# High table parts kept in PSUM for the subtraction, and part of the one-hot work of the first supertile given to ScalarE, in a recommendation-model tower on one core

## The chip, the core and the metric

The kernel runs on one core of a Trainium2 chip. TensorE (PE) does the matmuls, VectorE (DVE) and ScalarE (ACT) the elementwise work and the moves out of PSUM, GpSimd (POOL) gathers table rows with indirect DMAs, and SyncE (SP) issues most other DMAs. The metric is the device time of one execution in microseconds, the median of three runs.

## The reference

A batch of 2048 samples looks up one row of 128 numbers in each of 27 tables. All pairs of the 27 rows are multiplied (351 dot products), 16 dense values are appended, and three layers follow.

```
e = jnp.stack([tbl_0[ids[:, 0]], ..., tbl_26[ids[:, 26]]], axis=1)
dot = jnp.einsum('bnd,bmd->bnm', e, e)          # the 351 pairs are kept as z
h = jnp.concatenate([z, dense_ctx], axis=1)
h = jnp.maximum(h @ W_top1 + b_top1, 0.0)
h = jnp.maximum(h @ W_top2 + b_top2, 0.0)
y = h @ W_top3
```

## The kernel before

The batch is cut into NS = 4 supertiles of ST = 4 tiles of 128 samples. Ten small tables (eight of 1000 rows, two of 1250, the "hot" ones, numbered h = 0 to 9) are looked up on TensorE, for a whole supertile at a time: a table lies in SBUF with its rows on 125 partitions in 8 or 10 chunks, VectorE makes a one-hot matrix of 125x512 for each chunk (`tensor_scalar`, `is_equal`, L478), and TensorE multiplies the chunk with it (L664, L666). To keep fp32 accuracy a table is held as two parts of the type fp32r: `table_hi`, the table rounded by a cast on ScalarE (`split_high`, L527), and `table_lo`, the table minus `table_hi`, a `tensor_tensor` on VectorE (`split_low`, L444). Both are made once, in the first supertile, between the lookups. An eleventh table ("half", h = 10) is looked up in the same way with one-hots of 256 columns (L460, L681, L682), in the first two supertiles only. The other 16 tables (17 later on) are gathered on GpSimd, one indirect DMA for a table and tile (L434), into one of NR = 3 buffers; the gathers of tile k+3 wait for TensorE's transposes of tile k.

In a tile, TensorE transposes the gathered rows (L692), ScalarE and VectorE copy them into `eT` (L574, L494), TensorE forms the products of the pairs (L710) in four banks, `products(n, t, 0)` in the two `ps_hot` banks and `products(n, t, 1)` in the two `ps_dot` banks, and VectorE and ScalarE copy the banks out (L231). Layers of earlier tiles are woven in (L723, L745, L766).

What sets the order is the program text of each engine, with counting semaphores between engines:

- In the first supertile VectorE does for each hot table `split_low(h)` and then its 8 or 10 one-hots; it may be NO = 4 one-hots ahead of TensorE (`onehot_used`).
- ScalarE splits tables 0 to 3 ahead of the lookups. Then it copies the result of table h out of PSUM (L582) and splits table h + 4 behind that copy. TensorE has two PSUM banks for the lookups, and waits for the copy of table h before it begins table h + 2.
- A raw table h + 4 lands in the same place as table h (`PLACE`, four places), so SyncE issues its load (L304) when `split_low(h)` is done (`lo_ready`).

## Time and profile before

| | before |
|---|---|
| median of 3 runs | 641.28 us (640.8 to 643.16) |
| the profiled execution: its time | 642.85 us |
| the profiled execution: its span | 641.0 us |
| mean granted TensorE clock | 0.787 |
| busy: PE, DVE, ACT, POOL | 404.4, 215.7, 97.9, 260.6 us |

The profiled execution is one run; its span is what the trace covers, and its time is that of the run as it is timed. A busy share is an average over the whole span, and this kernel has stretches of very different kinds: the lookups of a supertile and its four tiles.

### The profile page before, as it was taken

How to read it: one execution, taken by the hardware profiler on the slowest of the kernel's cores; microseconds unless marked ns; L12 is line 12 of the kernel's file. 1: busy time of each engine (PE TensorE's matmuls, PEld its weight loads, DVE VectorE, ACT ScalarE, POOL GpSimd, SP SyncE). 2: the span in 40 equal slices, each digit the busy share in tenths (PEclk: the TensorE clock that was granted, in tenths of full speed). 3: DMA queues.
4: the chain of work that ended last, by engine and by line, in shares of the span. 5: the costliest groups of instructions: out<-in, count | busy, mean ns of one | idle time of the engine just before them, and what ended most of it. 6: DMA issues, size and time to landing. Idle time of an engine off the chain costs nothing.

```text
span 641.0 us, 9183 instructions
## 1 busy us (share of the span) xinstructions
PE 404.4 (63%) x3768; PEld 341.8 (53%) x3768; DVE 215.7 (34%) x462; ACT 97.9 (15%) x190; POOL 260.6 (41%) x272
## 2 busy tenths in 40 slices
PE   5888315263739992819271999371808089955997
PEld 3667204152628891718161888261707078845996
DVE  6898003010109960301010797010101059801220
ACT  2442001010111210102020212010201012110322
POOL 6778763544540027363645001737273600072000
PEclk9899557585959996758685999666767579985999
DMA  8983313131414202223222230123232325010322
GB/s 224 248 213 93 82 49 69 49 81 38 97 37 91 61 13 53 55 67 62 61 62 60 49 103 8 50 44 86 39 84 45 77 34 114 9 50 23 59 48 36
DMA packets 71137, 45.23 MB, mean 71 GB/s; under 512 B 53100, under 2 KB 59628, under 8 KB 71096
## 3 DMA queue, kind: packets, MB, share of 16 engines
q1 hardware_dynamic: 60578, 25.80, 18.0%
q0 software_dynamic: 8448, 17.32, 10.7%
q10 hardware_dynamic: 2070, 1.53, 1.0%
q8 instruction: 30, 0.49, 0.3%
q14 instruction: 11, 0.09, 0.0%
HBM read 38.75 MB, written 5.87 MB: 70 GB/s over the span
## 4 chain that ended last, share of the span: by engine, by line
PE 54%; issue 33%; DVE 4%; another core or an unknown queue 3%; DMA 3%; SPq 1%; ACT 1%; ACTq 0%
PE ps_hot L710 12%; PE ps_hot L664 10%; PE ps_hot L666 9%; PE ps_h L723 6%; PE ps_dot L710 6%; PE ps_tr L692 5%; PE ps_h L745 3%; DVE onehot L478 3%; DMA dots<-in_tbl 2%; PE ps_h L766 2%; PE ps_hot L681 1%; PE ps_hot L682 1%; DVE table_lo L444 1%; DMA dots_scratch<-dots 1%
## 5 line engine op out<-in xcount | busy, mean ns | idle before, releaser
L434 POOL DMA_INDIRECT rows<-in_tbl,cold_ids x264 | 259.7, 984 | 320.6 <-PE ps_tr L692 237.9
L710 PE MATMUL ps_hot<-eT 128*54 128x54 f32 x1024 | 77.2, 261 | 214.7 <-issue 195.3
L710 PEld LDWEIGHTS ps_hot<-eT 128*54 128x54 f32 x1024 | 59.1, 171 | 232.5 <-issue 211.9
L478 DVE TENSOR_SCALAR onehot<-hot_ids,row_number 125x512 fp32r<-125x512 int32 x336 | 146.8, 485 | 4.7 <-PE ps_hot L666 2.6
L664 PE MATMUL ps_hot<-onehot,table_hi 125*128 125x512 f32 x336 | 134.2, 399 | 14.8 <-DVE onehot L478 10.9
L666 PE MATMUL ps_hot<-onehot,table_lo 125*128 125x512 f32 x336 | 132.9, 396 | 0.0
L231 DVE COPY dots<-ps_hot 128x432 f32<-128x432 f32 x16 | 9.7, 608 | 238.3 <-remote 131.7
L664 PEld LDWEIGHTS ps_hot<-onehot,table_hi 125*128 125x128 f32 x336 | 64.2, 191 | 33.1 <-issue 17.6
L666 PEld LDWEIGHTS ps_hot<-onehot,table_lo 125*128 125x128 f32 x336 | 64.2, 191 | 13.1
L494 DVE COPY eT<-ps_tr 128x512 f32<-128x512 f32 (+1 forms) x36 | 23.3, 648 | 111.6 <-remote 56.4
L723 PE MATMUL ps_h<-zT,w 128*128 128x128 f32 x360 | 50.6, 281 | 0.0
L723 PEld LDWEIGHTS ps_h<-zT,w 128*128 128x128 f32 x360 | 46.0, 197 | 0.1
L582 ACT COPY eT<-ps_hot 128x512 f32<-128x512 f32 x40 | 26.6, 665 | 107.0 <-PE ps_hot L666 107.0
L692 PE MATMUL ps_tr<-ident,rows 128*128 128x128 f32 x264 | 41.8, 280 | 0.9 <-ACT eT L574 0.7
L710 PEld LDWEIGHTS ps_dot<-eT 128*54 128x54 f32 x1024 | 37.4, 164 | 6.2 <-issue 6.1
L710 PE MATMUL ps_dot<-eT 128*54 128x54 f32 x1024 | 39.4, 249 | 1.2 <-issue 1.2
L544 ACT ACTIVATE h<-ps_h,b 128x128 f32<-128x128 f32 x30 | 9.4, 363 | 159.5 <-remote 146.8
L692 PEld LDWEIGHTS ps_tr<-ident,rows 128*128 128x128 f32 x264 | 31.3, 144 | 3.3 <-ACT eT L574 1.4
L574 ACT COPY eT<-ps_tr 128x512 f32<-128x512 f32 (+1 forms) x36 | 20.1, 559 | 65.0 <-remote 39.1
L745 PE MATMUL ps_h<-h,w 128*128 128x128 f32 x240 | 29.4, 276 | 0.4 <-ACT results L554 0.4
L745 PEld LDWEIGHTS ps_h<-h,w 128*128 128x128 f32 x240 | 28.0, 192 | 0.8 <-ACT h L539 0.7
L231 DVE COPY dots<-ps_dot 128x432 f32<-128x432 f32 x16 | 9.7, 608 | 44.4 <-PE ps_dot L710 44.4
(39 smaller groups left out, 140.0 us busy)
## 6 DMA issues: line engine op xcount, KB each, us to landing
hot_ids<-in_hot_ids SPq DMA_DIRECT2D x40, 256.0 KB
dots_scratch<-dots SPq DMA_DIRECT2D x62, 87.8 KB
rows<-in_tbl,cold_ids POOLq DMA_INDIRECT x264
zT<-dots_scratch SPq DMA_DIRECT2D x47, 58.5 KB
w<-in_tbl SPq DMA_DIRECT2D x3, 448.0 KB
dots<-in_tbl SPq DMA_DIRECT2D x2, 560.0 KB
dots<-in_tbl SPq DMA_DIRECT2D x2, 448.0 KB
w<-in_tbl SPq DMA_DIRECT2D x1, 560.0 KB
```

What stands on the lines that cost most here:

```text
L231: return copy(dots[i][:, :, BS * k:BS * k + BS], of)
L434: pool.indirect_dma_start(out=rows[k % NR][:, f, :], out_offset=None, in_=x["cold"][f][:, :], in_offset=bass.IndirectOffsetOnAxis(ap=cold_ ...
L478: dve.tensor_scalar(onehot[:, c % NO, :], hot_ids[h % NI][0:CR, :], row, None, ALU.is_equal).then_inc(onehot_ready, 1)
L494: dve.tensor_copy(eT[:, i, :, at:at + len(f), :], ps_tr[1][:, 0:len(f), :].rearrange("d f (q b) -> d q f b", b=2))\
L574: act.copy(eT[:, t % 2, :, at:at + len(f), :], ps_tr[0][:, 0:len(f), :].rearrange("d f (q b) -> d q f b", b=2)).then_inc(tr_read[0], 1)
L582: act.copy(eT[:, :, :, NC + h:NC + h + NH + 1:NH, :], ps_hot[h % 2][:, :].rearrange("d (a i q b) -> d i q a b", a=2, i=2, b=2))\
L664: pe.matmul(ps_hot[h % 2][:, :], table_hi[:, c, :], onehot[:, c % NO, :], start=(c == FROM[h]), stop=False)
L666: pe.matmul(ps_hot[h % 2][:, :], table_lo[:, c, :], onehot[:, c % NO, :], start=False, stop=(c == FROM[h + 1] - 1)).then_inc(onehot_used, 1)
L692: last = pe.transpose(ps_tr[pair][:, f - TG * g, :], rows[tile(n, t) % NR][:, f, :], ident[:, :])
L710: last = pe.matmul(banks[k][SC * c:SC * c + WN, WN * g:WN * g + WN], e.rearrange("d a b -> d (a b)"), e.rearrange("d a b -> d b a"), start ...
L723: last = pe.matmul(ps_h1[:, m, :], w1[0:k, c, m * P:(m + 1) * P], zT[i][0:k, c, :], start=(c == 0), stop=(c == KC - 1))
L745: last = pe.matmul(ps_h2[:, m, :], w2[:, c, m * P:(m + 1) * P], h1[:, c, :], start=(c == 0), stop=(c == M1 - 1))
```

## The change

1. The eight PSUM banks are declared as `ps_hot` (two banks as before) and two tensors of three banks, `ps_tr_h1` and `ps_dot_h2`; `ps_tr`, `ps_dot`, `ps_h1` and `ps_h2` are views of them. In the first supertile, whose tiles have not begun, these two serve as two places (`apart`) for the high part of a table.
2. `split_high(h)` for h > 0 casts the staged table twice: into `table_hi` in SBUF, and into `apart[h % 2]` in PSUM. `split_low(h)` for h > 0 subtracts the PSUM copy instead of the one in SBUF. The second cast waits for `split_low(h - 2)`.
3. ScalarE splits tables 0 to 2 ahead of the lookups, and table h + 3 (not h + 4) behind the copy of table h.
4. In the first supertile the one-hot of the last chunk of tables 3 to 9 is made by ScalarE (`one_hot`): `Abs` of row number minus id into `distance` (the storage of `h1`), and then `Relu` of one minus that. It stands behind the copy of table h - 1 and ahead of the split of table h + 2, and its `Relu` waits for `onehot_used` of four chunks earlier. VectorE skips these seven chunks. SyncE's loads of ids into a used buffer wait for ScalarE's read too.
5. The two memsets of `ps_dot` on VectorE, and TensorE's wait for them, are gone; the copies of the products take 118 of 128 partitions.

```
-        ps_tr = [ps(f"ps_tr{i}", [P, TG, P]) for i in range(2)]
-        ps_dot = [ps(f"ps_dot{i}", [P, ST * P]) for i in range(2)]
-        ps_h1 = ps("ps_h1", [P, M1, P])
-        ps_h2 = ps("ps_h2", [P, 4, P])
+        ps_tr_h1 = ps("ps_tr_h1", [P, 3, 4, P])
+        ps_dot_h2 = ps("ps_dot_h2", [P, 3, 4, P])
+        apart = [bank.rearrange("p a c d -> p (a c) d")[0:CR] for bank in (ps_tr_h1, ps_dot_h2)]
...
             def split_low(h, part=0):
...
-                dve.tensor_tensor(in_table(table_lo, h, part), staging[h][:, a:b], in_table(table_hi, h, part),
+                high = apart[h % 2][:, 0:CHUNKS[h]] if h else in_table(table_hi, h, part)
+                dve.tensor_tensor(in_table(table_lo, h, part), staging[h][:, a:b], high,
                                   ALU.subtract).then_inc(lo_ready, 1)
...
+                        if by_scalar(n, c):
+                            continue
...
             def split_high(h, part=0):
...
-                act.copy(in_table(table_hi, h, part), staging[h][:, a:b]).then_inc(hi_ready, 1)
+                high = act.copy(in_table(table_hi, h, part), staging[h][:, a:b])
+                if h:
+                    if h > 2:
+                        act.wait_ge(lo_ready, splits(h - 2))
+                    high = act.copy(apart[h % 2][:, 0:CHUNKS[h]].bitcast(f32r), staging[h])
+                high.then_inc(hi_ready, 1)
...
+            def one_hot(h):
+                c = FROM[h + 1] - 1
+                row = row_number[0:CR, KINDS.index(CHUNKS[h]), CHUNKS[h] - 1:CHUNKS[h]]
+                act.wait_ge(hot_ids_ready[h % NI], 16 * (ids_uses(0, h) + 1))
+                act.wait_ge(act_onehot_ready, by_scalar_before(0, c))
+                act.activation(distance, hot_ids[h % NI][0:CR, :], ACT.Abs, bias=row, scale=-1.0)\
+                   .then_inc(distance_ready, 1)
+                act.wait_ge(distance_ready, by_scalar_before(0, c + 1))
+                act.wait_ge(onehot_used, c - NO + 1)
+                act.activation(onehot[:, c % NO, :], distance, ACT.Relu, bias=1.0, scale=-1.0)\
+                   .then_inc(act_onehot_ready, 1)
...
-                    if first and h + NB < NH:
-                        split_high(h + NB)
-                    if first and h == BEFORE[NH]:
-                        split_high(NH)
+                    if first and h + 1 in BY_SCALAR:
+                        one_hot(h + 1)
+                    if first and h + NB - 1 <= NH:
+                        split_high(h + NB - 1)
```

ScalarE's instructions from the splits ahead of the lookups on, before (`ps_hot0` and `ps_hot1` are the results of even and odd tables; `dots0`, `dots1`, `w2`, `w1` are the places of the raw tables):

```order
L527 CAST table_hi<-dots1 125x1024
L527 CAST table_hi<-w2 125x1024
L527 CAST table_hi<-w1 125x1024
L582 COPY eT<-ps_hot0 128x128x2x2
L527 CAST table_hi<-dots0 125x1024
L582 COPY eT<-ps_hot1 128x128x2x2
L527 CAST table_hi<-dots1 125x1024
L582 COPY eT<-ps_hot0 128x128x2x2
```

The same place in the changed kernel:

```order
L555 CAST ps_tr_h1<-w2 125x1024
L624 COPY eT<-ps_hot0 128x128x2x2
L551 CAST table_hi<-w1 125x1024
L555 CAST ps_dot_h2<-w1 125x1024
L624 COPY eT<-ps_hot1 128x128x2x2
L551 CAST table_hi<-dots0 125x1024
L555 CAST ps_tr_h1<-dots0 125x1024
L624 COPY eT<-ps_hot0 128x128x2x2
L612 ACTIVATE h1<-hot_ids3,row_number 125x512
L616 ACTIVATE onehot<-h1 125x512
L551 CAST table_hi<-dots1 125x1024
L555 CAST ps_dot_h2<-dots1 125x1024
```

The copy of table 1 (the first from `ps_hot1`) stood behind the cast of table 4 (`dots0`) and now stands ahead of it; each table has a second cast, and two activations stand between copy and casts from table 3 on.

VectorE's instructions at the same tables in the changed kernel, from `split_low(2)` on:

```order
L469 TENSOR_TENSOR table_lo<-w2,ps_tr_h1 125x1024
L505 TENSOR_SCALAR onehot<-hot_ids2,row_number 125x512 x8
L469 TENSOR_TENSOR table_lo<-w1,ps_dot_h2 125x1024
L505 TENSOR_SCALAR onehot<-hot_ids3,row_number 125x512 x7
L469 TENSOR_TENSOR table_lo<-dots0,ps_tr_h1 125x1024
L505 TENSOR_SCALAR onehot<-hot_ids0,row_number 125x512 x7
```

The order is that of before; the second input of each subtraction is in PSUM, and from table 3 on there is one one-hot fewer.

## Rows read from the trace of the kernel before

**Rows 1.** The profile page: busy time, share of the span and instructions

```profile
PE 404.4 (63%) x3768; PEld 341.8 (53%) x3768; DVE 215.7 (34%) x462; ACT 97.9 (15%) x190; POOL 260.6 (41%) x272
```

**Rows 2.** Timeline of VectorE, 0 to 64 us (start, duration, instruction, idle before)

```profile
31.94 1.21 DVE L444 TENSOR_TENSOR table_lo<-dots,table_hi 125x1024 fp32r<-125x1024 f32 x1
33.07 3.29 DVE L478 TENSOR_SCALAR onehot<-hot_ids,row_number 125x512 fp32r<-125x512 int32 x8
36.29 1.21 DVE L444 TENSOR_TENSOR table_lo<-w,table_hi 125x1024 fp32r<-125x1024 f32 x1
...
56.77 1.47 DVE L444 TENSOR_TENSOR table_lo<-w,table_hi 125x1280 fp32r<-125x1280 f32 x1
...
62.88 0.69 DVE L494 COPY eT<-ps_tr 128x512 f32<-128x512 f32 x1 [1.67 <-PE ps_tr L692]
```

**Rows 3.** Timeline of TensorE, 0 to 64 us

```profile
23.98 0.47 PE L664 MATMUL ps_hot<-onehot,table_hi 125*128 125x512 f32 x1 [1.86 <-ACT eT L582]
...
57.13 0.39 PE L666 MATMUL ps_hot<-onehot,table_lo 125*128 125x512 f32 x1
57.36 0.39 PE L664 MATMUL ps_hot<-onehot,table_hi 125*128 125x512 f32 x1
...
61.60 1.04 PE L692 MATMUL ps_tr<-ident,rows 128*128 128x128 f32 x8
```

**Rows 4.** Timeline of ScalarE, 0 to 64 us

```profile
15.35 2.00 ACT L527 CAST table_hi<-w 125x1024 fp32r<-125x1024 f32 x2 [4.72 <-DMA w<-in_tbl]
...
22.32 1.05 ACT L527 CAST table_hi<-dots 125x1024 fp32r<-125x1024 f32 x1 [4.45 <-DMA dots<-in_tbl]
23.27 0.61 ACT L582 COPY eT<-ps_hot 128x512 f32<-128x512 f32 x1
...
39.28 1.27 ACT L527 CAST table_hi<-dots 125x1280 fp32r<-125x1280 f32 x1 [3.17 <-DMA dots<-in_tbl]
```

**Rows 5.** Timeline of GpSimd, 0 to 141 us: single gathers

```profile
11.62 2.41 POOL L434 DMA_INDIRECT rows<-in_tbl,cold_ids  x1 [0.30 <-issue]
...
31.65 1.18 POOL L434 DMA_INDIRECT rows<-in_tbl,cold_ids  x1 [0.30 <-issue]
...
41.71 1.62 POOL L434 DMA_INDIRECT rows<-in_tbl,cold_ids  x1 [0.30 <-issue]
...
51.28 2.25 POOL L434 DMA_INDIRECT rows<-in_tbl,cold_ids  x1 [0.30 <-issue]
53.84 1.28 POOL L434 DMA_INDIRECT rows<-in_tbl,cold_ids  x1 [0.30 <-issue]
...
56.91 2.16 POOL L434 DMA_INDIRECT rows<-in_tbl,cold_ids  x1 [0.30 <-issue]
...
74.36 0.94 POOL L434 DMA_INDIRECT rows<-in_tbl,cold_ids  x1 [0.30 <-issue]
...
93.08 0.94 POOL L434 DMA_INDIRECT rows<-in_tbl,cold_ids  x1 [0.30 <-issue]
103.97 0.94 POOL L434 DMA_INDIRECT rows<-in_tbl,cold_ids  x1 [9.95 <-PE ps_tr L692]
...
122.70 0.94 POOL L434 DMA_INDIRECT rows<-in_tbl,cold_ids  x1 [0.30 <-issue]
```

**Rows 6.** Groups on GpSimd, 12 to 56.8 us (count, busy, mean ns, idle before)

```profile
L434 POOL DMA_INDIRECT rows<-in_tbl,cold_ids x29 | 36.4, 1257 | 8.8 <-issue 8.8
```

**Rows 7.** Groups on GpSimd, 61.8 to 94 us

```profile
L434 POOL DMA_INDIRECT rows<-in_tbl,cold_ids x26 | 24.5, 943 | 7.9 <-issue 7.9
```

**Rows 8.** Timeline of VectorE, 60 to 165 us: copies of the first product bank

```profile
96.88 0.61 DVE L231 COPY dots<-ps_hot 128x432 f32<-128x432 f32 x1 [31.09 <-remote]
...
127.49 0.61 DVE L231 COPY dots<-ps_hot 128x432 f32<-128x432 f32 x1 [19.18 <-remote]
```

**Rows 9.** Timeline of VectorE, 595 to 625 us: the same copy without gathers

```profile
598.55 0.61 DVE L231 COPY dots<-ps_hot 128x432 f32<-128x432 f32 x1 [2.56 <-PE ps_hot L710]
```

**Rows 10.** Busy time by engine, clock, DMA share and GB/s, 35 to 40 us

```profile
35.00:40.00 5.00, 4.56 (x20) 3.46 (x19) 5.00 (x12) 1.83 (x3) 4.08 (x4) 1.00 1.04 228
```

38 lines of the change are left out of this document (28 added, 10 removed).

## The prediction

> **What bounds the kernel now.** I began with the busy shares of the page. They name no bound: PE is busy for 63% of the span, POOL for 41%, DVE for 34% [rows 1]. So I went by stretches of time, and read the timelines of the engines beside each other.
>
> The first stretch is the lookups of the first supertile, up to 61.6 us, where the transposes of tile 0 begin [rows 3]. VectorE is the engine without gaps there. One table of 1000 rows takes it from 31.94 to 36.29, 4.35 us: a subtraction that holds it for 1.13 us (31.94 to 33.07) and eight one-hots in 3.22 us, 0.40 us each [rows 2]. TensorE has a matmul every 0.23 us (57.13 to 57.36), so 0.46 us for the two of a chunk and 3.7 us for eight [rows 3]: it is the faster of the two, by 0.6 us a table. ScalarE mostly waits for raw tables to land: 4.45 us before 22.32, 3.17 us before 39.28 [rows 4]. The DMA engines are fully busy until then (a share of 1.04 from 35 to 40 us) [rows 10].
>
> The second stretch is tile 0, and here the reader must look twice. TensorE's first products are listed from 66 us on, but VectorE, which copies the first bank when it is complete, does so only at 96.88, after 31.09 us of idling [rows 8]. Nothing that the trace names holds TensorE meanwhile. What runs all that time is GpSimd: its last gather begins at 93.08 and ends at 94.02, then it idles for 9.95 us until the transposes of tile 1 let it go on [rows 5]. The bank is copied 2.9 us behind the end of the gathers. In tile 1 the last gather ends at 123.64 [rows 5] and the copy comes at 127.49 [rows 8], 3.9 us behind. In a tile beside which nothing is gathered VectorE idles for 2.56 us before the same copy [rows 9]. So the first products of a tile end when the gathers beside them end, whatever the mechanism is. I take this as an empirical rule, shown by these rows as a coincidence in time and not yet as a cause.
>
> It follows that the time of tile 0's products is set by how fast GpSimd gets through its first 64 gathers, from 3.8 to 94.0 us, without one wait for anybody. From tile 1 on, gathers start with a tile's transposes (103.97) [rows 5] and products end with the gathers; that alternation has no slack, so what tile 0 gains should reach the end in full.
>
> **GpSimd's pace.** Alone, a gather takes 0.94 us and comes every 1.25 us [rows 7, 5]. While VectorE works on the lookups the mean is 1.257 us for 29 gathers [rows 6], 0.31 us more each. Beside one-hots it is up to 1.28 us (53.84) [rows 5]. Four are far longer: 2.41 us at 11.62, 1.62 at 41.71, 2.25 at 51.28 and 2.16 at 56.91 [rows 5]. The last ends 0.8 us behind the subtraction of 56.77 to 58.24 [rows 2], so it seems to have waited for it.
>
> **The change, part by part.**
>
> *The subtraction from PSUM.* If it is the second SBUF input that shuts GpSimd out, the four long gathers shrink to the 1.28 us of a gather beside one-hots: 1.13 + 0.34 + 0.97 + 0.88 = 3.3 us. Other gathers that start inside a subtraction lose 0.2 to 0.3 us now; two or three of these make 0.5 us. The trace has no subtraction with an input in PSUM. VectorE's copy of 512 columns from PSUM takes 0.69 us [rows 2], and 512 more columns cost the subtraction about what they should (1.21 us for 1024), so I take it as unchanged; bounds are 0 and 0.15 us each (1.4 us for ten).
> The Trainium skill (SBUF — State Buffer, section "Who interferes with whom") says that a VectorE instruction with two SBUF inputs contends with a GpSimd instruction that reads SBUF and one with a single SBUF input does not; a gather reads its ids from SBUF, and the long gathers agree. The same section says that tensor_tensor was not seen to stall descriptor generation, by which these 3.8 us would be nothing.
>
> *Seven one-hots fewer on VectorE.* 7 x 0.40 = 2.8 us [rows 2].
>
> *The order on ScalarE.* TensorE idled 1.86 us at 23.98 for the copy of table 1 [rows 3], which stood behind the cast of table 4 and its landing at 22.3 [rows 4]. Now the copy goes first. VectorE had been held by that too, being four one-hots ahead at most. Against it: table 2 lands at 15.3 and now needs two casts of 1.0 us (the two casts at 15.35 took 2.00 [rows 4]) before VectorE may subtract, at 17.35 where it did at 16.4: 0.9 us lost.
>
> I follow VectorE through the tables. Subtraction 2 at 17.35, then 1.13 + 8 x 0.40 = 4.3 us: subtraction 3 at 21.65. From there 1.13 + 7 x 0.40 = 3.93 us a table: 25.6, 29.5, 33.4, 37.4, 41.3 for tables 4 to 8. Table 8 lands at 39.3 and won't land earlier, since the DMA engines are full [rows 10]; two casts of 1.2 us [rows 4] give 41.6. Then 1.40 + 9 x 0.40 = 5.0 us each: 46.6 for table 9, 51.6 for the half table, against 56.77 now [rows 2]. The transposes of tile 0 begin near 56.4 in place of 61.6, 5.2 us earlier.
>
> *ScalarE's load.* A table costs a copy of 0.61 us, two casts of 1.0 us, and two activations of 512 columns, for which the trace has no row; the copy of 512 columns, 0.61 us [rows 4], is the nearest, and the bounds are 0.5 and 1.0 us. That is 3.8 us of the 3.93 us that VectorE takes: nearly full, but it fits. Its Relu waits until half of the table is used and TensorE needs it 1.4 us after that. Behind it stand the casts, needed a table later, and the copy, needed when TensorE begins the table after next. A hiccup of about 1 us is likely at table 8, whose landing holds ScalarE; VectorE's four one-hots of lead cover it.
>
> *The memsets.* 1.0 us on VectorE before any table has landed; nothing.
>
> *The sum.* With VectorE through 5.2 us sooner, that much of GpSimd's time runs at 1.25 us a gather and not at about 1.5: 5.2 x 0.25 / 1.5 = 0.9 us. Together 3.3 + 0.5 + 0.9 = 4.7 us. GpSimd's gathers of tile 3 (the first at 74.36 [rows 5]) come after the transposes with 8 us to spare, so no wait enters. If my rule of the gathers were wrong and products simply followed lookups, the gain would be the 5.2 us; the two readings hardly differ in their result. The profiled execution would go from 642.85 us (span 641.0) to 638.2 (span 636.3); it lay 1.6 us above the median, so for the median 641.28 - 4.7 = 636.6 us.
>
> **The rivals.**
>
> *The gathers are not relieved (chance 0.2).* The subtraction holds GpSimd wherever its second input lies, or GpSimd's long gathers have another reason. For it: the gather at 31.65 [rows 5] meets the subtraction that begins at 31.94 [rows 2] and takes 1.18 us only. Then only the 0.9 us of the earlier end counts, 1.5 us if some one-hots' locks go too: 639.8 to 640.4 us, within 0.5%.
>
> *ScalarE becomes the bound of the lookups, but the gathers hide it (0.06).* With activations of 1.0 us its lap is 4.6 us, the lookups end about where they do now, and since GpSimd still profits from the subtraction, the time is 638 to 639.
>
> *Slower (0.06).* The mechanism is ScalarE again, further on. Its Relu, casts and copy are one queue, and TensorE needs a piece of it for each table. The lookups may end 8 us later than I forecast without harm, at about 65 us; beyond 69.7 us the gathers of tile 3 (74.36 less 4.7) wait for tile 0's transposes and everything moves. That needs a lap of some 6 us. A lap of 7 us (3.1 us more for each of seven tables) puts the lookups' end at 78, the gathers of tile 3 behind it at 80 where they now begin at 74.4, and the time at 641.3 + 5.6 = 647 us. Against it: only two instructions of 512 columns are new to the trace.
>
> **How the numbers follow.** A difference of 0.5% is 3.2 us, about what a measurement of this kernel can tell from none: 638.1 us is the border. The forecast (0.68) has its own range of 634.5 to 638.6: 3.4 us of it is the long gathers, where the phase between gathers and subtractions decides, and runs of before spread over 2.4 us. The range up to 640.8 takes in the unrelieved gathers and leaves out little more than the slower case and the tail below. Of the forecast 0.62 lies beyond 0.5%, and of the ScalarE rival 0.03: faster 0.65, same 0.27, slower 0.08 (with 0.02 for a clock or DMA shift that I don't see).
>
> **What would show it.** In the profile after: subtractions still 1.2 us; no gather above 1.3 us from 12 us on; TensorE's idle time at 23.98 gone; the half table's subtraction at 51.6 and tile 0's transposes at 56.4; the last of the first 64 gathers over at 89.3 and the first product bank copied at 92.2. If that copy comes 2.9 us behind the gathers again, the rule held. The forecast fails if long gathers stay beside the subtractions, or if later tiles take the gain back in a wait of their own.

## The result, and the profile of the changed kernel

The changed kernel is slower. Its median is 657.14 us (654.32 to 663.23 in 6 runs) against 642.05 us (640.8 to 643.94 in 6 runs) for the kernel before, measured together: a ratio of 1.0242 [1.0206, 1.0278]. The forecast was 636.6 us. The profiled execution took 656.15 us, with a span of 654.3 us. Medians and ranges have every run, the ratios leave out those over 1.5% above the fastest run of the same kernel. Runs of this kernel scatter more than those of the kernel before (8.9 us here, against 3.1), and on some chips more than on others; the experiments show that this scatter is part of the answer.

The page gives the busy times, and they tell little:

```profile
PE 407.9 (62%) x3768; PEld 339.3 (52%) x3768; DVE 213.0 (33%) x453; ACT 116.4 (18%) x214; POOL 255.3 (39%) x272
```

Against [rows 1] VectorE has nine instructions fewer, ScalarE 24 more, and GpSimd needs 5.3 us less for the same 272. TensorE has the same instructions. Again one has to go by stretches, and the first of them, the lookups, is where the kernels part.

VectorE's timeline of the changed kernel there (start, duration, instruction, idle time before it and its releaser):

```profile
34.00 1.22 DVE L469 TENSOR_TENSOR table_lo<-w,ps_tr_h 125x1024 fp32r<-125x1024 f32 x1
...
39.02 0.49 DVE L505 TENSOR_SCALAR onehot<-hot_ids,row_number 125x512 fp32r<-125x512 int32 x1 [0.94 <-PE ps_hot L712]
40.42 0.49 DVE L505 TENSOR_SCALAR onehot<-hot_ids,row_number 125x512 fp32r<-125x512 int32 x1 [0.91 <-issue]
...
68.08 0.49 DVE L505 TENSOR_SCALAR onehot<-hot_ids,row_number 125x512 fp32r<-125x512 int32 x1 [4.44 <-remote]
71.59 0.49 DVE L505 TENSOR_SCALAR onehot<-hot_ids,row_number 125x512 fp32r<-125x512 int32 x1 [3.02 <-remote]
72.00 1.48 DVE L469 TENSOR_TENSOR table_lo<-dots,ps_tr_h 125x1280 fp32r<-125x1280 f32 x1
```

Until 34 us VectorE is within 0.6 us of the forecast. Then its one-hots come 1.4 us apart and later 4.9 us apart, where [rows 2] have one every 0.40 us. The first rows name TensorE as the releaser, and "remote" is one that the trace doesn't resolve. TensorE in the same stretch:

```profile
49.06 0.77 PE L710 MATMUL ps_hot<-onehot,table_hi 125*128 125x512 f32 x1 [0.94 <-DVE onehot L505]
...
58.74 0.79 PE L710 MATMUL ps_hot<-onehot,table_hi 125*128 125x512 f32 x1 [2.29 <-issue]
...
63.70 0.80 PE L710 MATMUL ps_hot<-onehot,table_hi 125*128 125x512 f32 x1 [3.74 <-issue]
...
68.63 0.80 PE L710 MATMUL ps_hot<-onehot,table_hi 125*128 125x512 f32 x1 [3.71 <-issue]
...
77.17 0.39 PE L710 MATMUL ps_hot<-onehot,table_hi 125*128 125x512 f32 x1
77.62 0.40 PE L710 MATMUL ps_hot<-onehot,table_hi 125*128 125x512 f32 x1
...
88.21 1.04 PE L738 MATMUL ps_tr_h<-ident,rows 128*128 128x128 f32 x8
```

A chunk takes up to 4.96 us, and what TensorE waits for is "issue": nothing that the trace names. By 77 us the matmuls from `table_hi` come every 0.45 us again.

Which engine waits for which? The named releasers mislead, and counting settles it: the trace has all 84 one-hots of the first supertile (77 of VectorE, 7 of ScalarE) and their 84 pairs of matmuls, so the one-hot of each chunk can be found. The one that begins at 63.16 is for chunk 60 (counted from 0). Its buffer was last read for chunk 56, by the pair of matmuls from 49.06 on, which is over at 50.26. So the buffer was free 12.9 us before VectorE wrote it. TensorE's matmul for chunk 60 begins at 63.70, 0.05 us behind the end of that one-hot (63.65), and it is 0.05 or 0.06 us for each of chunks 57 to 62. In this stretch TensorE waits for VectorE, and VectorE for nothing that its program asks for. Its one-hots from 51.85 on start 2.82, 3.53, 4.96, 4.92 and 3.51 us apart, which is close to 4, 5, 7, 7 and 5 times 0.70 us. ScalarE is late too:

```profile
73.05 0.63 ACT L616 ACTIVATE onehot<-h 125x512 fp32r<-125x512 f32 x1 [13.62 <-remote]
```

This `Relu` needs the end of the matmuls of chunk 59 (59.96) and of its own `Abs` (59.43), and it begins 13.1 us later; TensorE's next matmul begins when it is done, at 73.73.

Nor is it TensorE's clock. From 36 to 44 us, when the one-hots are already 1.4 us apart, the granted clock is 0.93; TensorE has 14 matmuls there, and 31 in the 8 us before. At the clock of 0.50 a chunk takes 0.86 us (74.75 to 75.61).

The transposes of tile 0 begin at 88.21, where they began at 61.60 [rows 3]: 26.6 us late. GpSimd tells when the bad stretch ends:

```profile
67.32 0.95 POOL L458 DMA_INDIRECT rows<-in_tbl,cold_ids  x1 [0.31 <-issue]
89.08 0.94 POOL L458 DMA_INDIRECT rows<-in_tbl,cold_ids  x1 [20.82 <-PE ps_tr_h L738]
...
107.84 0.95 POOL L458 DMA_INDIRECT rows<-in_tbl,cold_ids  x1 [0.31 <-issue]
116.04 0.94 POOL L458 DMA_INDIRECT rows<-in_tbl,cold_ids  x1 [7.25 <-PE ps_tr_h L738]
```

The row at 67.32 is the 48th gather, the last that needs no transposes. It is over at 68.27, and VectorE and TensorE recover 3 to 4 us later. GpSimd then waits 20.82 us for the transposes of tile 0: its gathers of tile 3 begin at 89.08, where they began at 74.36 [rows 5], 14.7 us late. This wait is how the loss reaches the end. The table by stretches says it in one line (busy time and count of TensorE, weight loads, VectorE, ScalarE, GpSimd; clock, DMA share, GB/s):

```profile
44.00:72.00 28.00, 9.74 (x16) 4.02 (x16) 5.14 (x10) 4.13 (x5) 18.47 (x20) 0.50 0.32 87
```

In 28 us TensorE ran 16 matmuls, at a granted clock of 0.50 (1.2 GHz of 2.4).

**How 26.6 us become 13.3.** The kernel before has such a stretch too, only later. Its weight loads in tile 0's products, which run beside the same gathers:

```profile
84.17 0.16 PEld L710 LDWEIGHTS ps_hot<-eT 128*54 128x54 f32 x1 [2.63 <-issue]
84.90 0.17 PEld L710 LDWEIGHTS ps_hot<-eT 128*54 128x54 f32 x1 [0.57 <-issue]
87.70 0.17 PEld L710 LDWEIGHTS ps_hot<-eT 128*54 128x54 f32 x1 [2.63 <-issue]
90.50 0.16 PEld L710 LDWEIGHTS ps_hot<-eT 128*54 128x54 f32 x1 [2.63 <-issue]
```

```profile
86.30 0.25 PE L710 MATMUL ps_hot<-eT 128*54 128x54 f32 x1 [1.80 <-issue]
```

The loads start 0.73, 2.80 and 2.80 us apart, which is close to one and four times 0.70 us, and the matmul of a load comes 1.40 us behind it. No record is missing: the trace has all 64 loads and all 64 matmuls of this bank. The first 39 matmuls run at full pace, in 2.28 us from 66.00 on, with the same gathers beside them, and only then do the steps begin (in the changed kernel it is 42, from 91.69 on). It looks as if instructions reached the engine only at moments 0.70 us apart, a few or none at a time. I call this the **slow supply**. It is what the prediction saw as 31.09 us of VectorE's idling [rows 8] and tied to the gathers without a cause. In the changed kernel the slow supply began in the lookups. So 16 of the first 64 gathers were left for tile 0's products, where 26 ran behind that point before [rows 7]. From tile 0's transposes to the first gather of tile 1's, 88.21 to 116.04 is 27.8 us, and 61.60 to 103.97 [rows 3, 5] was 42.4 us. Of the 26.6 us lost 14.5 came back, 12.1 stayed at 116.04, and the span is 13.3 us longer. The lookups had slack: they may end until the gathers of tile 3 are due.

### The profile page after: what moved, and what is told of

The parts are those of the page before. It is cut to its first block, busy times and chain, and to the rows that moved or that the text cites. A ratio compares the mean times of both kernels' runs of the same rounds, so it can differ in the third digit from the quotient of the medians.

```text
span 654.3 us, 9217 instructions
## 1 busy us (share of the span) xinstructions
PE 407.9 (62%) x3768; PEld 339.3 (52%) x3768; DVE 213.0 (33%) x453; ACT 116.4 (18%) x214; POOL 255.3 (39%) x272
## 4 chain that ended last, share of the span: by engine, by line
PE 56%; issue 31%; another core or an unknown queue 7%; DMA 3%; ACT 2%; DVE 0%; SPq 0%; ACTq 0%
PE ps_hot L710 12%; PE ps_hot L712 11%; PE ps_hot L754 11%; PE ps_tr_h L767 6%; PE ps_dot_h L754 5%; PE ps_tr_h L738 4%; PE ps_dot_h L789 3%; DMA w<-in_tbl 2%; PE ps_dot_h L810 2%; PE ps_hot L727 1%; PE ps_hot L728 1%; DMA dots_scratch<-dots 1%; ACT eT L603 0%; DMA zT<-dots_scratch 0%
## 5 line engine op out<-in xcount | busy, mean ns | idle before, releaser
L521 DVE COPY eT<-ps_tr_h 128x512 f32<-128x512 f32 (+1 forms) x36 | 23.3, 648 | 118.7 <-remote 58.4
L767 PE MATMUL ps_tr_h<-zT,w 128*128 128x128 f32 x360 | 51.4, 284 | 0.0
L767 PEld LDWEIGHTS ps_tr_h<-zT,w 128*128 128x128 f32 x360 | 46.7, 200 | 0.8 <-issue 0.7
L754 PE MATMUL ps_dot_h<-eT 128*54 128x54 f32 x1024 | 39.1, 241 | 7.4 <-issue 7.4
L754 PEld LDWEIGHTS ps_dot_h<-eT 128*54 128x54 f32 x1024 | 36.2, 156 | 13.2 <-issue 13.1
L738 PE MATMUL ps_tr_h<-ident,rows 128*128 128x128 f32 x264 | 40.9, 276 | 0.7 <-ACT eT L603 0.5
L738 PEld LDWEIGHTS ps_tr_h<-ident,rows 128*128 128x128 f32 x264 | 30.5, 141 | 2.9 <-issue 1.0
L603 ACT COPY eT<-ps_tr_h 128x512 f32<-128x512 f32 (+1 forms) x36 | 20.1, 560 | 62.7 <-remote 36.0
L789 PE MATMUL ps_dot_h<-h,w 128*128 128x128 f32 x240 | 29.4, 276 | 0.4 <-ACT results L583 0.4
L789 PEld LDWEIGHTS ps_dot_h<-h,w 128*128 128x128 f32 x240 | 28.0, 192 | 0.8 <-ACT h L568 0.7
```

Source lines behind the costliest of these rows:

```text
L521: dve.tensor_copy(eT[:, i, :, at:at + len(f), :], ps_tr[1][:, 0:len(f), :].rearrange("d f (q b) -> d q f b", b=2))\
L603: act.copy(eT[:, t % 2, :, at:at + len(f), :], ps_tr[0][:, 0:len(f), :].rearrange("d f (q b) -> d q f b", b=2)).then_inc(tr_read[0], 1)
L738: last = pe.transpose(ps_tr[pair][:, f - TG * g, :], rows[tile(n, t) % NR][:, f, :], ident[:, :])
L754: last = pe.matmul(banks[k][SC * c:SC * c + WN, WN * g:WN * g + WN], e.rearrange("d a b -> d (a b)"), e.rearrange("d a b -> d b a"), start ...
L767: last = pe.matmul(ps_h1[:, m, :], w1[0:k, c, m * P:(m + 1) * P], zT[i][0:k, c, :], start=(c == 0), stop=(c == KC - 1))
L789: last = pe.matmul(ps_h2[:, m, :], w2[:, c, m * P:(m + 1) * P], h1[:, c, :], start=(c == 0), stop=(c == M1 - 1))
```

## The experiments

The kernels of one call run on the same chip and are compared with runs of the kernel before on that chip. This matters more than I knew when I began: on two of the chips the kernel before takes 640 to 644 us (medians), on two others 381 to 382 us. Which chip the first measurement ran on isn't recorded. A time is comparable within its group only.

### Which part of the change brings the slow supply into the lookups

Four kernels in one group; the kernel before has a median of 644.24 us here (638.18 to 650.84, 19 runs).

**e_psum**: subtraction from PSUM and the new order, but all one-hots on VectorE.

```
-BY_SCALAR = range(3, NH)
+BY_SCALAR = range(0, 0)
```

> The changed kernel with all one-hots made by VectorE again; the second cast into PSUM, the subtraction from PSUM and the new split order stay. Theory A (TensorE falls into a state of one instruction every 0.7 us beside gathers as soon as its lookups run without the small waits that VectorE's pace gave it, whoever makes the one-hots): the slow stretch in the lookups appears only if TensorE's pace of before is exceeded; here VectorE is again at 4.35 us a table, so no slow stretch, lookups over at 59 to 60 us, gathers relieved, 635 to 639 us. Theory B (ScalarE's one-hot starts it): the same 635 to 639 us. Theory C (PSUM traffic of the casts beside TensorE starts it): slow stretch stays, 650 to 660 us.

Measured: 667.62 us (665.92 to 671.77), ratio 1.0376 [1.0319, 1.0433]. VectorE's timeline of this kernel:

```profile
24.24 0.50 DVE L505 TENSOR_SCALAR onehot<-hot_ids,row_number 125x512 fp32r<-125x512 int32 x1 [0.56 <-PE ps_hot L712]
...
36.25 1.20 DVE L469 TENSOR_TENSOR table_lo<-dots,ps_tr_h 125x1024 fp32r<-125x1024 f32 x1
...
70.50 1.22 DVE L469 TENSOR_TENSOR table_lo<-dots,ps_dot_h 125x1024 fp32r<-125x1024 f32 x1
```

The slow supply begins between 21 and 28 us (one-hots 1.4 us apart at 21.38, 22.80 and 24.24, waits that grow from 27.85 on), 8 to 15 us sooner than in the changed kernel, and the two subtractions of tables 4 and 5 lie 34 us apart. Again it ends about 4 us behind the 48th gather (over at 66.3). ScalarE makes no one-hot here, so its one-hots aren't the cause, and VectorE's pace at the start is that of the kernel before, so theory A fails with theory B. GpSimd's gathers of tile 3 wait longer still:

```profile
102.03 0.94 POOL L458 DMA_INDIRECT rows<-in_tbl,cold_ids  x1 [35.70 <-PE ps_tr_h L738]
```

**e_onehot**: ScalarE's one-hots and the new order, but the subtraction from SBUF as before, with the two memsets back on VectorE.

```
-                high = apart[h % 2][:, 0:CHUNKS[h]] if h else in_table(table_hi, h, part)
-                dve.tensor_tensor(in_table(table_lo, h, part), staging[h][:, a:b], high,
+                dve.tensor_tensor(in_table(table_lo, h, part), staging[h][:, a:b], in_table(table_hi, h, part),
...
-                if h:
-                    if h > 2:
-                        act.wait_ge(lo_ready, splits(h - 2))
-                    high = act.copy(apart[h % 2][:, 0:CHUNKS[h]].bitcast(f32r), staging[h])
```

> The changed kernel without the PSUM copies: the subtraction reads table_hi in SBUF again, one cast a table, memsets and the wait for them back; ScalarE's seven one-hots and the new split order stay. Theories A and B: the slow stretch in the lookups stays, 650 to 660 us. Theory C (PSUM traffic): it is gone, 637 to 641 us.

Measured: 646.62 us (644.89 to 649.45), ratio 1.0038 [1.0007, 1.0068].

**e_three**: both of these edits at once, so that only the new order of ScalarE's splits and the layout of PSUM remain.

> Only the new split order (table h + 3 behind the copy of table h) and the layout of PSUM; no PSUM copies, no one-hots on ScalarE. All theories: no slow stretch in the lookups; TensorE's 1.86 us wait for the copy of table 1 is gone; lookups over 1 to 2 us earlier; time within 2 us of before, 639 to 642 us, since the first product bank waits for the gathers. If the slow stretch is here, the order alone starts it: 650 us or more.

Measured: 644.51 us (641.21 to 648.1), ratio 1.0009 [0.9979, 1.0039]. VectorE's subtraction of the half table and its copy of the first product bank in e_onehot:

```profile
52.23 1.48 DVE L468 TENSOR_TENSOR table_lo<-w,table_hi 125x1280 fp32r<-125x1280 f32 x1
...
100.19 0.61 DVE L241 COPY dots<-ps_hot 118x432 f32<-118x432 f32 x1 [37.48 <-remote]
```

In e_three the same two rows are at 53.59 and 102.16, the second with 39.53 us of idling before it. Neither profile has the slow supply in its lookups; in the kernel before the half table is at 56.77 [rows 2]. But the first bank is no earlier than 96.88 [rows 8]. Lookups that end 4.5 and 3.2 us sooner gave nothing: they only lengthened the idling before that copy (37.48 and 39.53 us against 31.09). The first 64 gathers were over no sooner either, at 94.5 and 97.1 us against 94.0, since the subtractions held GpSimd as before.

**e_hold2**: the changed kernel, in which GpSimd begins the gathers of tile 2 only after the last subtraction. It was to show what happens to a slow stretch in the lookups when gathers stop in it.

```
+                if k == 2:
+                    pool.wait_ge(lo_ready, splits(NH))
```

> The changed kernel, but GpSimd waits for the last subtraction of the lookups before the 16 gathers of tile 2. If the end of the gathers ends the slow stretch, TensorE is at full pace again about 3.7 us behind gather 32 (near 47 to 51 us and not 72), and the slow stretch of tile 0 lasts until the 32 gathers behind it are done, some 20 us longer; the total is then 645 to 665 us. If it ends for a reason of its own in TensorE's or ScalarE's program, it lasts until 70 us or more as in the changed kernel.

Measured: 645.84 us in a single run, with no interval. VectorE just before the hold takes effect:

```profile
50.31 0.49 DVE L507 TENSOR_SCALAR onehot<-hot_ids,row_number 125x512 fp32r<-125x512 int32 x1 [0.53 <-issue]
51.71 2.86 DVE L507 TENSOR_SCALAR onehot<-hot_ids,row_number 125x512 fp32r<-125x512 int32 x7 [0.92 <-PE ps_hot L714]
```

Only two one-hots come late, 1.40 us apart, around the end of gather 32 (50.15), and from 51.71 on seven come at full pace. It looks like a slow supply that began near 50 us and ended 1.6 us after the gathers stopped, but two rows are too little to answer the question with. The run shows something else: up to 49 us the changed kernel had no slow supply in its lookups, and it doesn't always get it there.

What follows from the four: the PSUM half of the change (the second copy of the high part and the subtraction that reads it) brings the slow supply forward. That was theory C in direction, though all three times lie above its ranges (e_psum at 667.62 us most of all). The rest of the change does little: e_onehot is at most 0.7% slower, e_three can't be told from the kernel before.

### Does the slow supply need the gathers, and their pace?

The theories here are P, by which it needs gathers that come at their free pace, every 1.25 us, and G, by which any gathers will do. Two kernels take gathers away or space them in the changed kernel, two space them in the kernel before. In **e_plain** the rows of tiles 1 and 2 come in plain loads from SyncE; these are the first 128 rows of each table and not the gathered ones, so the kernel computes with other rows there.

```
+                    if k in (1, 2):
+                        continue
...
+                    for k in (1, 2):
+                        for f in range(NC - 1):
+                            sp.dma_start(rows[k][:, f, :], x["cold"][f][0:P, :])\
+                              .then_inc(plain_ready[k - 1][f // TG // BACK], 16)
```

In **e_fill_first** (the changed kernel), **e_fill1** and **e_fill3** (the kernel before) GpSimd writes 256 unused columns behind a gather, so that the next one comes later: in e_fill_first once behind each of the first 48 gathers (tiles 0 to 2, as below), in e_fill1 once behind each gather from the 49th on (`k >= NR`), in e_fill3 three times.

```
+                    for _ in range(1 if k < NR else 0):
+                        pool.wait_ge(filled, fills)
+                        pool.memset(idle[:, :], 0.0).then_inc(filled, 1)
+                        fills += 1
```

> The changed kernel with the 32 gathers of tiles 1 and 2 replaced by plain loads of the first 128 rows of each table from SyncE (so those tiles compute with other rows than asked for). GpSimd gathers for tile 0 alone (16 gathers, over near 25 us) until the lookups end. If GpSimd's gathers are what TensorE's slow stretch needs, the lookups have none: the half table's subtraction at 51 to 54 us, transposes of tile 0 at 56 to 59 us, and tile 0's first bank is copied 3 to 6 us behind its 16 gathers, near 82 us; total 622 to 632 us. If the slow stretch belongs to the PSUM traffic alone, it stays and the total is above 650 us.

> The changed kernel with one memset of 256 columns on GpSimd behind each of the first 48 gathers, so that they come every 1.6 us or so instead of every 1.25. If the slow stretch is entered because gathers run at their free pace (theory P, pace), it is gone: lookups over at 56 to 58 us; the 64 gathers then end near 100 us and the total is 643 to 648 us. If any gathers beside the PSUM subtraction do it (theory G), the slow stretch stays and is longer, over only near 85 us: 665 us or more.

> The kernel before, with one memset of 256 columns on GpSimd behind each gather from tile 3's on (pitch about 1.6 us instead of 1.25). Theory P: TensorE no longer slows down in the products, the first bank is copied within 5 us of the transposes while gathers still run, and tiles are then paced by GpSimd alone: 560 to 630 us. Theory G: products still end with the gathers, each tile with gathers beside it is 5 to 6 us longer: 700 to 725 us.

> The same with three memsets behind each gather from tile 3's on (pitch about 2.4 us). Theory P: no slow stretch, GpSimd's pace alone: 201 gathers and more at 2.4 us, 620 to 680 us. Theory G: products end with the gathers, 18 us more in each of 12 tiles: 830 to 870 us.

This group ran on a chip where the kernel before takes 380.93 us (379.82 to 384.87, 7 runs), which none of the expectations had foreseen. There is no slow supply on it, so P and G can't be told apart there. The times are 368.99 us for e_plain (ratio 0.9709 [0.964, 0.9778]), 385.43 for e_fill_first (1.0135 [1.0084, 1.0186]), 427.14 for e_fill1 (1.1207 [1.1165, 1.125]) and 598.95 for e_fill3 (1.5696 [1.5629, 1.5763]). GpSimd is the bound there, with 83% of the chain in e_fill3. In e_fill1 216 gathers have a memset behind them; at the 0.20 us by which one memset widens the pitch (below) that is 43 us by estimate, and the time rose by 46.

I repeated two of them, with both kernels, on a chip of the other kind: the kernel before is at 640.8 us (638.28 to 645.83, 25 runs) in this group. **c_before** and **c_after** are the two kernels unchanged, **c_fill_first** and **c_plain** are e_fill_first and e_plain.

> The kernel before, unchanged, profiled in the same call as the next three, because the last call's runs of before took 381 us where the earlier ones took 641 to 644. If this call's times are near 381 us, its trace has no stretch in which TensorE issues an instruction every 0.7 us, and the first product bank is copied at 61 to 70 us; if they are near 642 us, it is the trace of before over again. Its ratio to before is 1.00 either way.

> The changed kernel, unchanged. Theory S (the loss comes only from the slow instruction supply beside gathers): where before takes 381 us, the lookups end 4 to 5 us sooner and nothing is given back, 375 to 378 us; where before takes 642 us, 655 to 660 us as first measured. Rival (a wait of the change's own, ScalarE's queue, costs time wherever it runs): at least 383 us beside 381 us.

> The changed kernel with one memset on GpSimd behind each of the first 48 gathers, again. Beside 642 us for before: theory P (free pace of the gathers starts the slow supply) has no slow stretch in the lookups and 643 to 650 us; theory G (any gathers do) 665 us or more. Beside 381 us: 385 us as in the last call.

> The changed kernel with plain loads in place of the gathers of tiles 1 and 2 (those tiles compute with other rows), again. Beside 642 us for before: without gathers beside the lookups no slow stretch there, lookups over at 56 to 59 us, 622 to 632 us in all. If it is slow all the same, gathers are not what starts it. Beside 381 us: 369 us as in the last call.

c_before took 641.3 us (637.52 to 645.28), ratio 0.9991 [0.9953, 1.0029]. c_after took 641.75 us (639.24 to 655.66), ratio 1.0007 [0.9971, 1.0044]: on this chip the changed kernel makes no difference, and only one of its ten runs took over 650 us. The 655 to 660 us that theory S had called for beside 642 us did not come. Its profile shows the case in which the slow supply stays out of the lookups. VectorE:

```profile
33.12 1.21 DVE L469 TENSOR_TENSOR table_lo<-w,ps_tr_h 125x1024 fp32r<-125x1024 f32 x1
37.02 1.21 DVE L469 TENSOR_TENSOR table_lo<-w,ps_dot_h 125x1024 fp32r<-125x1024 f32 x1
...
51.13 1.48 DVE L469 TENSOR_TENSOR table_lo<-w,ps_tr_h 125x1280 fp32r<-125x1280 f32 x1
...
96.29 0.61 DVE L241 COPY dots<-ps_hot 118x432 f32<-118x432 f32 x1 [26.82 <-remote]
```

GpSimd, the last of the first 64 gathers:

```profile
89.85 0.95 POOL L458 DMA_INDIRECT rows<-in_tbl,cold_ids  x1 [0.31 <-issue]
```

And TensorE, at the transposes of tile 0:

```profile
55.82 1.04 PE L738 MATMUL ps_tr_h<-ident,rows 128*128 128x128 f32 x8
60.24 1.11 PE L738 MATMUL ps_tr_h<-ident,rows 128*128 128x128 f32 x4 [3.38 <-issue]
```

The lookups end 5.8 us sooner, and at once the slow supply begins, at 57 us in the transposes, where in the kernel before it began in the products, behind the first 39 of them.

c_fill_first took 638.53 us (637.88 to 642.85), ratio 0.997 [0.9942, 0.9998], below the 643 to 650 us of P and far from the 665 us of G. Its gathers come every 1.6 us in the lookups and every 1.45 us behind them, VectorE's half table is at 58.73 (no slow supply in the lookups), and its first bank is copied at 71.28, 25.6 us sooner than 96.88 [rows 8]. GpSimd, VectorE and the table by stretches of this kernel:

```profile
50.80 0.95 POOL L461 DMA_INDIRECT rows<-in_tbl,cold_ids  x1 [0.16 <-issue]
51.75 0.50 POOL L467 MEMSET idle<- 128x256 f32 x1
```

```profile
53.84 4.97 DVE L512 TENSOR_SCALAR onehot<-hot_ids,row_number 125x512 fp32r<-125x512 int32 x9
58.73 1.47 DVE L476 TENSOR_TENSOR table_lo<-w,ps_tr_h 125x1280 fp32r<-125x1280 f32 x1
...
71.28 0.61 DVE L243 COPY dots<-ps_hot 118x432 f32<-118x432 f32 x1 [4.16 <-remote]
```

```profile
66.00:79.00 13.00, 7.90 (x120) 5.70 (x118) 1.30 (x2) 0.94 (x2) 11.21 (x19) 0.75 0.28 74
79.00:98.00 19.00, 4.17 (x21) 2.33 (x20) 0.61 (x1) 0.00 (x0) 14.14 (x15) 0.50 0.20 52
```

The last memset is over at 77.57. Up to there, with spaced gathers, TensorE gets through its work at 120 matmuls in 13 us (from 69 us on three to six products every 0.72 us or so). Behind it, with gathers every 1.25 us, it has 21 in 19 us. This is the clearest sign that the pace of the gathers sets how slow the supply is.

What the run doesn't show is that the pace decides whether the slow supply enters the lookups. It still does all the PSUM work of the change without a slow supply there, but on this chip so did c_after, unspaced, in its profile and by its times in nine of ten runs. And the memsets change VectorE too: nine one-hots take 4.97 us, where c_after has 3.66 us at the same table, so its lap is 4.66 us (27.80 to 32.46), longer than in the kernel before. Spaced gathers and slower lookups come together here.

c_plain took 623.33 us (620.96 to 624.28), ratio 0.9709 [0.965, 0.9769], as expected. It has no gathers from about 26 us to 57.16, and no slow supply in that time (nor had c_after on this chip, with gathers). The supply is slow soon after gathers run again, from 61 us on:

```profile
57.16 0.94 POOL L465 DMA_INDIRECT rows<-in_tbl,cold_ids  x1 [30.81 <-PE ps_tr_h L748]
...
75.87 0.94 POOL L465 DMA_INDIRECT rows<-in_tbl,cold_ids  x1 [0.30 <-issue]
```

```profile
80.86 0.61 DVE L242 COPY dots<-ps_dot_h 118x432 f32<-118x432 f32 x1 [13.11 <-PE ps_dot_h L764]
```

The 16 gathers end at 76.8 and tile 0's second bank is copied 4.0 us later. With fewer gathers beside it, tile 0 was done 19.8 us sooner than in the kernel before (the first gather that waits for tile 1's transposes starts at 84.14 against 103.97 [rows 5]), and 17.5 us are left of it at the end. From the transposes of tile 0 (56.28) that is 27.9 us with 16 gathers, as in the changed kernel (27.8 us, 16 gathers), against 42.4 us with 26 in the kernel before. So the time that the slow supply costs falls with the number of gathers beside a tile, and in no profile was there a slow supply more than 5.5 us after they had stopped. No run tells the instructions of the gathers on GpSimd from the transfers that they start.

### The change where there is no slow supply

Four kernels on another chip of the faster kind; the kernel before has a median of 382.28 us here (379.64 to 384.93, 16 runs). **d_after** is the changed kernel, **d_psum** is e_psum, **d_fill1** is e_fill1, and **d_fill_all** is the changed kernel with one such memset behind every gather.

> The changed kernel, unchanged, a third time. First it took 657 us beside 642, then 642 beside 641. Theory V (the slow supply is entered at no fixed place in the program, and the changed kernel's lookups, with GpSimd unhindered by the subtractions, only make an early entry likely): times spread from 638 to 663 us, the profiled run slow from somewhere between 30 and 75 us on. Rival (each chip has its one behaviour): all runs within 1% of each other. Beside 381 us for before: 375 to 378 us.

> The changed kernel with all one-hots on VectorE, again, first 668 us beside 644. Theory V: 640 to 670 us, slow stretch in the lookups where the time is above 650 us. Beside 381 us for before: 376 to 380 us.

> The kernel before with one memset behind each gather from tile 3's on, again. It took 427 us on a chip where before takes 381 us. Beside 641 us for before: theory P (the free pace of the gathers starts the slow supply, and 1.6 us between gathers avoids it) 430 to 520 us; theory G (any gathers do): products still end with the gathers, 700 to 725 us.

> The changed kernel with one memset behind every gather. Theory P: no slow stretch at all, 430 to 520 us beside 641 us for before, and 425 to 432 us beside 381 us. Theory G: 700 us or more beside 641 us.

d_after took 377.94 us (376.01 to 382.0), ratio 0.9888 [0.985, 0.9927]: 4.3 us less, in the 375 to 378 us expected. d_psum took 376.91 us, ratio 0.986 [0.9801, 0.9918], so the PSUM half alone gives the gain, and ScalarE's one-hots add nothing that can be told. d_fill1 took 428.97 us (1.1215 [1.1154, 1.1277]) and d_fill_all 432.82 us (1.1305 [1.1246, 1.1363]): memsets cost 12 to 13% here. The page of d_after, its busy times and the chain that ended last:

```profile
PE 345.3 (92%) x3768; PEld 300.2 (80%) x3768; DVE 212.3 (57%) x453; ACT 116.5 (31%) x214; POOL 267.0 (71%) x272
POOL 69%; issue 21%; PE 4%; DMA 3%; ACT 1%; ACTq 1%; POOLq 0%; SPq 0%
```

GpSimd is the bound of this program. TensorE's products of tile 0:

```profile
62.83 1.87 PE L754 MATMUL ps_hot<-eT 128*54 128x54 f32 x64 [0.94 <-ACT eT L603]
```

The 64 products of a bank take 1.87 us, and VectorE copies the first bank at 63.98. In the kernel before on the other kind of chip the same 64 take 31.8 us (66.00 to 97.75), with gathers beside them too.

### Spaced gathers where there is a slow supply

Two kernels on the chip of the first group; the kernel before is at 639.67 us (638.12 to 644.36, 11 runs). **g_after** is the changed kernel, **g_fill1** is e_fill1, the kernel before with one memset behind each gather but the first 48.

> The changed kernel, unchanged, a fourth time. Beside 640 to 644 us for before: theory V again, runs spread over 638 to 663 us, those with the slow stretch in the lookups above 650 us. Beside 381 us: 376 to 379 us, as in the third.

> The kernel before with one memset behind each gather from tile 3's on. Twice it ran beside 381 us for before (427 and 429 us). Beside 641 us: theory P (the gathers' free pace starts the slow supply) 430 to 520 us; theory G (any gathers do, and it ends with them) 700 to 725 us. Beside 381 us: 427 to 429 us again.

g_after has a median of 651.83 us with six runs from 641.12 to 659.46 (642.81, 659.46, 641.12, 651.32, 658.24, 652.34); for so wide a scatter no ratio is given. The profiled one is that of 642.81 us, in which the one-hots come late from 52 us on, so that the half table is subtracted at 55.61, and not at 51.13 as in c_after, and the transposes of tile 0 begin at 74.21. So here too the slow supply is in the lookups, for their last 20 us, and costs nothing, because GpSimd has hardly to wait:

```profile
75.54 0.94 POOL L458 DMA_INDIRECT rows<-in_tbl,cold_ids  x1 [4.05 <-PE ps_tr_h L738]
```

These gathers of tile 3 begin 1.2 us behind those of the kernel before (74.36 [rows 5]); in the first measurement it was 14.7 us, and in e_psum 27.7 us. The times are longer by 3.1 us here, 15.1 us and 23.4 us (profiled 642.81 us and medians 657.14 and 667.62, against the medians of before). The same program on the same chip takes 641 or 659 us. That the longer runs differ from the profiled one by an earlier start of the slow supply is likely but inferred, since none of them was profiled.

g_fill1 took 614.38 us (612.75 to 615.41), ratio 0.9593 [0.9553, 0.9634]. P had called for 430 to 520 us and G for 700 to 725, so both are wrong in their pure form. Tile 1 in this kernel, gathers and copies:

```profile
103.22 0.95 POOL L437 DMA_INDIRECT rows<-in_tbl,cold_ids  x1 [6.24 <-PE ps_tr L699]
...
104.67 0.95 POOL L437 DMA_INDIRECT rows<-in_tbl,cold_ids  x1 [0.16 <-issue]
```

```profile
115.98 0.61 DVE L233 COPY dots<-ps_hot 128x432 f32<-128x432 f32 x1 [8.24 <-remote]
```

With a gather every 1.45 us rather than 1.25 the first bank is done 12.8 us behind the first gather, in the middle of the 16 gathers (the last is over at 126.04); in the kernel before it was done 23.5 us behind it (103.97 to 127.49 [rows 5, 8]). The supply is still slow, but less so: three or four products come every 1.4 us. This kernel is the fastest of those that do the whole work on a chip of this kind, by 4%, and is 12% slower on one of the other kind.

## Why the prediction was wrong, point by point

**The parts that held.** The price of each edit was right. TensorE's wait of 1.86 us at 23.98 is gone (in c_after its longest there is 0.41 us). Subtractions from PSUM take 1.21 and 1.48 us, those of before 1.21 and 1.47 [rows 2]. VectorE's lap is 3.90 us (33.12 to 37.02 in c_after), forecast 3.93. The half table's subtraction came at 51.13 in c_after, forecast 51.6; in d_after it came at 54.56, since ScalarE held VectorE up by 1.22 us at table 8 (the hiccup that I had held to be covered) and tables 8 and 9 took longer. No gather beside a subtraction from PSUM was long in any profile, where [rows 5] had four of 1.62 to 2.41 us. A few long ones are left beside one-hots: 1.68 us in c_after at 48.85, 2.35 us at 13.67 and 2.90 us at 34.85 in g_after, 2.35 us in e_hold2. From 12 to 51 us the mean gather took 1158 ns in c_after, 1108 in d_after and 1200 in g_after, against 1220 ns in the kernel before. The first 64 gathers were over at 90.8 us in c_after and at 89.3 in d_after, forecast 89.3. So the rival by which the subtraction holds GpSimd wherever its input lies is refuted, and the relief is of varying size. The Trainium skill (SBUF — State Buffer, section "Who interferes with whom") says that a VectorE instruction contends with a reading GpSimd instruction by its second SBUF input, and the rows agree; an instruction with one SBUF input is free of it outside the modes with two ports only, a condition that the prediction left out. What the section says of tensor_tensor not stalling descriptor generation doesn't hold for these gathers. And where GpSimd bounds the program the sum came out as well: 4.3 us measured, 4.7 forecast. That is in part luck, since the forecast was for another kind of chip, no trace of the kernel before was taken on this one, and d_psum gained 5.4 us without the one-hots on ScalarE.

**The step that failed in the first measurement** is VectorE's path through the tables: a lap of 3.93 us for each, and "the transposes of tile 0 begin near 56.4 in place of 61.6, 5.2 us earlier". It took for granted that the engines get their instructions as they did, with gathers at a freer pace beside them. They began at 88.21, since the slow supply was in the lookups from 36 us on; GpSimd waited 20.82 us for them, and the span grew by 13.3 us.

**A second step failed where the lookups did end early** (c_after, e_onehot, e_three), and it is the last before GpSimd's pace: "that alternation has no slack, so what tile 0 gains should reach the end in full", with the rule under it that "the first products of a tile end when the gathers beside them end". The rule described a coincidence in two tiles, and I took the stall for a fixed item of the products. It is a condition that comes with gathers, can begin before the products, and lasts until a few us after the gathers pause. Three readings show it. In e_onehot and e_three the lookups ended sooner and the first bank was no earlier. In c_after the gathers ended 3.2 us sooner than in the kernel before (90.8 against 94.0 [rows 5]) and the copy was 5.5 us behind them instead of 2.9, so only 0.6 us of it reached 96.29. And in g_fill1 and c_fill_first the first bank is done long before the gathers end.

**What put the time on the other side** is that the condition began in the lookups, which no rival of mine allowed for. It began between 21 and 28 us in e_psum, at about 36 us in the first profile of the changed kernel and at 52 us in that of g_after. By the times it came early enough to cost something in every run of e_psum and in some of the changed kernel (all six of the first measurement, one of ten in c_after, four of six in g_after). Why the PSUM half brings it there isn't shown. The gathers that VectorE used to hold up (1257 ns in the mean [rows 6]) come more evenly, every 1.25 to 1.6 us, and since their pace sets how slow the supply is (c_fill_first, g_fill1), it may also set where it begins. But no run with spaced gathers was made on a chip and in a group where the unspaced kernel had the slow supply early, and the added traffic to PSUM is the rival that stands untested.

**The rival for slower** had the path right and its start wrong. It said that lookups that end too late make the gathers of tile 3 wait for tile 0's transposes, and that the time grows by that wait. With these gathers at 89.08 in place of 74.36 its sum gives 641.3 + 14.7 = 656.0 us, and the profiled run took 656.15. But it named ScalarE's queue as what would delay the lookups. Its two activations take 0.72 and 0.64 us, inside the bounds given, its lap is about 4.0 us, and in the bad stretch it is late like the others (13.62 us of idling before its Relu at 73.05) and holds TensorE for under 1 us (0.97 at 46.90, 0.38 at 73.73). The chance of 0.08 for slower was too low, above all because the largest idle time of the profile, 31.09 us, had no cause that I knew; an unexplained stall in the middle of the argument should have kept both signs open.

**What stays open.** What makes the supply slow isn't shown. VectorE and ScalarE (in the lookups) and TensorE (in the products) get their instructions late, so it isn't a matter of one engine's work. The transfers that fetch instructions are not larger: on the page of the changed kernel and of d_after they read

```profile
q8 instruction: 30, 0.49, 0.3%
```

```profile
q8 instruction: 30, 0.49, 0.5%
```

which are the same 30 packets and, as shares of 16 engines in 654.3 and 374.2 us, about 31 and 30 us of packet time. The Trainium skill (Runtime: NRT & Kernel Launch, section "Instruction fetch mechanics") says that a sequencer fetches blocks of 256 instructions ahead of use. By that a late block would give one pause in 256 instructions and not one before every few, as the rows show. Why two chips have no slow supply, and why the same program meets it at 36 us in one run and at 57 in another, stays open too; no edit that I had could be tried against either.

## What to carry to other kernels

When an engine idles for tens of us and no row names a releaser, find out what it hangs on before pricing an edit next to it: take away or space what runs beside it, one run each. Relieving an engine that isn't the bound can make the whole slower, since its neighbours then meet it at another pace; here the relief is worth 1.1 to 1.4% where GpSimd is the bound (d_after, d_psum), and the same edit costs up to 2.4 and 3.8% where it isn't (the first measurement, e_psum). When two engines pass buffers to each other, count buffers before believing a named releaser: here the row said that VectorE waited for TensorE, and it was the other way round. And measure on more than one chip: the same two kernels compare as 1.024, 1.001 and 0.989 in three measurements.

## What the runs showed of the hardware

- On two chips (the one of the first and the last group, and the one of the c_ kernels) instructions of TensorE, VectorE and ScalarE came late, the first two in steps of about 0.7 us, while indirect gathers ran, from some moment on until 2 to 5.5 us after the gathers paused. On two others nothing of the kind is seen in the same program, and it takes 381 to 382 us instead of 640 to 644.
- The slow stretch from 44 to 72 us of the changed kernel has a granted clock of 0.50 (1.2 GHz) throughout, with 16 matmuls in 28 us. It had begun at a clock of 0.93 (36 to 44 us). The mean clock is 0.778 over its span, and 0.991 in d_after.
- A subtraction of 1024 or 1280 columns costs the same with its second input in PSUM as in SBUF (1.21 and 1.48 us), and GpSimd's gathers beside it are relieved: from 12 to 51 us 1158 ns in the mean (c_after) against 1220 ns (before).
- Gathers spaced by a memset of 0.33 us, 1.45 us apart, make the slow supply milder, for 4% of the whole time (g_fill1). Within c_fill_first TensorE had 120 matmuls in 13 us beside spaced gathers and 21 in 19 us behind the last memset.
- Such memsets hold VectorE's one-hots up: nine took 4.97 us beside them (c_fill_first) and 3.66 us without (c_after).
